# Products with values issued for four exponent steps at a time, in a fused attention and feed-forward layer

## What is computed

```python
qkv = x @ Wqkv + bqkv                      # 16 query heads of 16, 4 key/value heads of 16
scores = einsum('bqhd,bkhd->bhqk', q, k) / HD
prob = softmax(scores)
out = einsum('bhqk,bkhd->bqhd', prob, v).reshape(b, s, D)
x = layernorm(x + out @ Wout + bout)
gate, up = split(x @ ternary(w_gate_up).T) # 1024 hidden features
h = rms_norm(silu(gate) * up)
x = layernorm(x + h @ ternary(w_proj).T)
```

## Time and profile before

| | us |
|---|---|
| median of 3 runs | 574.95 (574.88 to 575.57) |
| the profiled execution's own time | 574.5 |
| its span, first to last instruction | 571.8 |
| PE busy in it | 528.4 (92%) |
| DVE busy | 455.4 (80%) |
| ACT busy | 374.2 (65%) |
| POOL busy | 319.5 (56%) |

### The profile page before, as it was taken

One profiled execution on the slowest core, in us unless ns is written; L12 is line 12 of the kernel. 1 busy time (PEld: TensorE's weight loads), 2 busy tenths in 40 slices (PEclk: granted clock), 3 DMA queues, 4 the chain that ended last, 5 costly groups with the idle time before them and its releaser, 6 DMA issues.

```text
span 571.8 us, 13792 instructions
## 1 busy us (share of the span) xinstructions
PE 528.4 (92%) x4176; PEld 444.7 (78%) x4176; DVE 455.4 (80%) x1025; ACT 374.2 (65%) x754; POOL 319.5 (56%) x478
## 2 busy tenths in 40 slices
PE   6497999999999999999999999999999999999883
PEld 5386778778888787878888888878887877787772
DVE  6878877788888888888888887888898888885764
ACT  5456755666767767676776776776767676667663
POOL 5577671255645555555646564556555565466764
PEclk9899999999999999999999999999999999999998
DMA  7865444343333426062534444261606253010001
GB/s 229 144 142 95 86 95 104 74 91 88 84 95 93 105 68 128 19 160 26 128 69 102 93 94 100 79 116 56 134 6 166 29 125 71 12 44 6 19 20 37
DMA packets 53931, 49.05 MB, mean 86 GB/s; under 512 B 6144, under 2 KB 53888, under 8 KB 53888
## 3 DMA queue, kind: packets, MB, share of 16 engines
q1 hardware_dynamic: 53200, 48.13, 38.2%
q10 hardware_dynamic: 688, 0.39, 0.2%
HBM read 33.29 MB, written 14.68 MB: 84 GB/s over the span
## 4 chain that ended last, share of the span: by engine, by line
PE 63%; DVE 20%; issue 7%; POOL 4%; ACT 2%; DMA 2%; SPq 0%; DVEq 0%; ACTq 0%; POOLq 0%
PE ffn_ps L551 19%; PE short_ps L477 10%; PE pv_ps L579 8%; PE short_ps L523 8%; PE down_ps L564 7%; PE exp_ps L532 6%; DVE row_max L800 5%; DVE gated L863 3%; DVE h_f L870 3%; PE short_ps L587 2%; DVE attB L902 2%; DVE pvT L896 1%; DVE w_hat L833 1%; POOL sq_sum L966 1%; DVE w_sum L821 1%
## 5 line engine op out<-in xcount | busy, mean ns | idle before, releaser
L800 DVE TENSOR_REDUCE row_max<-short_ps 128x2 f32<-128x512 f32 x256 | 173.4, 681 | 67.2 <-PE short_ps L523 66.8
L961 POOL TENSOR_TENSOR h_lo<-h_f,h_hi 128x256 fp32r<-128x256 f32 x128 | 94.8, 740 | 206.9 <-ACT h_hi L698 206.8
L722 ACT ACTIVATE probs<-exp_ps 128x1024 f32<-128x1024 f32 x128 | 130.7, 1021 | 34.1 <-PE exp_ps L532 33.2
L523 PE MATMUL short_ps<-k_st,q_st 65*128 65x256 f32 x512 | 108.2, 294 | 9.3 <-DVE v_ones L919 6.2
L523 PEld LDWEIGHTS short_ps<-k_st,q_st 65*128 65x128 f32 x512 | 87.9, 192 | 20.7 <-issue 7.8
L707 ACT ACTIVATE tanh<-ffn_ps 128x256 f32<-128x256 f32 x120 | 45.5, 380 | 85.2 <-PE ffn_ps L551 85.2
L551 PE MATMUL ffn_ps<-x1T_hi,wguT 128*128 128x256 f32 x480 | 82.0, 293 | 10.3 <-DVE h_f L870 8.9
L564 PE MATMUL down_ps<-wpT,h_hi 128*128 128x256 f32 x256 | 78.7, 330 | 3.8 <-POOL h_lo L961 3.8
L532 PE MATMUL exp_ps<-q_st,k_st 67*128 67x512 f32 x256 | 80.7, 397 | 0.8 <-DMA q_st<-shift_lo 0.6
L551 PEld LDWEIGHTS ffn_ps<-x1T_hi,wguT 128*128 128x128 f32 x480 | 64.8, 189 | 19.3 <-issue 9.7
L966 POOL TENSOR_TENSOR sq_sum<-sq_sum,h_sq 128x256 f32<-128x256 f32 x105 | 79.5, 758 | 0.0
(11 more groups left out here) (102 smaller groups left out, 830.7 us busy)
## 6 DMA issues: line engine op xcount, KB each, us to landing
q_st<-q_dram SPq DMA_DIRECT2D x128, 128.0 KB, 4.1
q_dram<-q_p SPq DMA_DIRECT2D x16, 512.0 KB, 3.0
xn<-in_L_attn_x_dram SPq DMA_DIRECT2D x16, 256.0 KB, 3.4
k_st<-k_dram SPq DMA_DIRECT2D x64, 64.0 KB, 2.8
res<-in_L_attn_x_dram SPq DMA_DIRECT2D x16, 256.0 KB, 2.9
out_dram<-y_out SPq DMA_DIRECT2D x16, 256.0 KB, 2.9
wgu_raw<-in_L_ffn_w_gate_up_dram SPq DMA_DIRECT2D x8, 256.0 KB, 6.6
k_dram<-k_p SPq DMA_DIRECT2D x16, 128.0 KB, 2.4
```

The source lines that it names most:

```text
L523: last = pe.matmul(bank[:, t * S:(t + 1) * S], q_st[0:PAD, st.par, head, t * P:(t + 1) * P], k_st[0:PAD, st.par, st.s % 4, :], start=True, ...
L722: act.activation(probs[:, st.s % 4], exp_ps[:], ACT.Exp).then_inc(exp_done, 1)
L800: dve.tensor_reduce(row_max[:, st.par, head * TT:(head + 1) * TT], short(n, f"max{i}")[:].rearrange("p (t k) -> p t k", t=TT), AX.X, ALU.m ...
L961: pool.tensor_tensor(h_p[1][:, st.s % 4, :], h_f[:, st.s % 2, :], h_p[0][:, st.s % 4, :].bitcast(F32), ALU.subtract).then_inc(h_lo, 1)
```

## The change

`probs` gets eight buffers, one for each step of a sequence. `times_v` is called at s = 3 and s = 7 only and does the work of four steps in one go: first steps s-3 and s-2, then s-1 and s, each as before. The products of steps 0 and 1 move from position 1 to position 3, those of steps 4 and 5 from position 5 to position 7. The semaphore `pv_done` counts two calls for each sequence in place of four, and the waits on it are rewritten for that. To make room on chip, eight buffers of the feed-forward and output stages (`tanh`, `gated`, `h_f`, `h_sq`, `y_sb`, `r2` and the two of `y_out`) are laid into `wgu_raw`, which held the weights as they were read.

```diff
-        probs = sb("probs", [P, 4, TT, 2, S])
+        probs = sb("probs", [P, SLOTS, TT, 2, S])
-        tanh = sb("tanh", [P, 2, S])
-        gated = sb("gated", [P, 2, S])
-        h_f = sb("h_f", [P, 2, S])
+
+        tanh, gated, h_f, h_sq, y_sb, r2, y_even, y_odd = (wgu_raw[:, 2 * i:2 * i + 2, :] for i in range(8))
+        y_out = (y_even, y_odd)
@@ times_v
-                if st.s % 4 == 1:
-                    wait(pe, pv_turned, st.count(2, st.s // 4))
-                for t in range(TT):
-                    for s in (st.s - 1, st.s):
-                        for i in range(2):
-                            r = 32 * quadrant(s % 4, i)
-                            last = pe.matmul(pv_ps[r:r + 32, s % 4 // 2, :], v_ones[:, st.par, t, s % 4, :],
-                                             probs[:, s % 4, t, i, :], start=(t == 0), stop=(t == TT - 1),
-                                             tile_position=(0, r))
+                wait(pe, pv_turned, st.count(2, st.s // 4))
+                for first in (st.s - 3, st.s - 1):
+                    for t in range(TT):
+                        for s in (first, first + 1):
+                            for i in range(2):
+                                r = 32 * quadrant(s % 4, i)
+                                last = pe.matmul(pv_ps[r:r + 32, s % 4 // 2, :], v_ones[:, st.par, t, s % 4, :],
+                                                 probs[:, s, t, i, :], start=(t == 0), stop=(t == TT - 1),
+                                                 tile_position=(0, r))
                 last.then_inc(pv_done, 1)
@@ PE's slot
-                if (st := n.chunk(PV0)) and st.s % 2:
+                if (st := n.chunk(PV0)) and st.s % 4 == 3:
                     times_v(st)
@@ ACT's slot
-                    wait(act, pv_done, st.count(4, st.s // 2 - 1))
-                    act.activation(probs[:, st.s % 4], exp_ps[:], ACT.Exp).then_inc(exp_done, 1)
+                    wait(act, pv_done, st.count(2, st.s // 4 - 1))
+                    act.activation(probs[:, st.s], exp_ps[:], ACT.Exp).then_inc(exp_done, 1)
@@ DVE's slot
-                        wait(dve, pv_done, st.count(4, 2 * half + 2))
+                        wait(dve, pv_done, st.count(2, half + 1))
-                    wait(dve, pv_done, st.count(4, -4))
+                    wait(dve, pv_done, st.count(2, -2))
```

More of the change, by code:

```diff
@@ L274, in postln_layer @@
         x1T = [sb(f"x1T_{n}", [P, 2, DT, S], F32R) for n in ("hi", "lo")]
-        tanh = sb("tanh", [P, 2, S])
-        gated = sb("gated", [P, 2, S])
-        h_f = sb("h_f", [P, 2, S])
+        tanh, gated, h_f, h_sq, y_sb, r2, y_even, y_odd = (wgu_raw[:, 2 * i:2 * i + 2, :] for i in range(8))
+        y_out = (y_even, y_odd)
         h_p = [sb(f"h_{n}", [P, 4, S], F32R) for n in ("hi", "lo")]
-        h_sq = sb("h_sq", [P, 2, S])
         sq_sum = sb("sq_sum", [P, 2, S])
-        y_sb = sb("y_sb", [P, TT, D])
         ms = sb("ms", [P, TT])
         inv = sb("inv", [P, TT])
-        r2 = sb("r2", [P, TT, D])
         st2 = sb("st2", [P, TT, 6])
@@ L290, in postln_layer @@
         mean2 = sb("mean2", [P, TT])
-        y_out = sb("y_out", [P, 2, TT, D])
         exp_ps = ps("exp_ps", [P, TT, 2 * S])
@@ L450, in slot @@
                     sp_wait(y_done, st.count(TT, TT))
-                    sp.dma_start(out[st.seq()].rearrange("(t p) d -> p t d", p=P), y_out[:, st.par]
+                    sp.dma_start(out[st.seq()].rearrange("(t p) d -> p t d", p=P), y_out[st.par]
                                  ).then_inc(stored[st.par], 16)
@@ L712, in slot @@
                     for t in range(TT):
-                        act.activation(y_out[:, st.par, t, :], r2[:, t, :], ACT.Identity, bias=shift2[:, t:t + 1],
+                        act.activation(y_out[st.par][:, t, :], r2[:, t, :], ACT.Identity, bias=shift2[:, t:t + 1],
                                        scale=rstd2[:, t:t + 1]).then_inc(y_done, 1)
```

## The result

The changed kernel takes 602.4 us (599.57 to 602.7, 4 runs) where the kernel before takes 574.91 in the same rounds: slower by 4.6%, ratio 1.046, 95% interval 1.0434 to 1.0485. The forecast was 598.4 with a range from 588 to 603. The profiled execution took 602.7, its span is 600.0, so 28.2 more than the span before.

The account below looks back on a forecast made before the run. PE bounds most of the cycle, DVE two stretches per sequence (from max0 at positions 4 and 0). 20.7 - 1.2 + 2.9 + 1.0 = 23.4 on the profiled 574.5 gives 597.9; with 0.45 for the median, 598.4, range 588 to 603.

Parts of the forecast that it names:

- The steady state: Twelve sequences, 100 to 475 us: 24 additions of 0.86 at positions 3 and 7, +20.7; 1.2 back at position 1.
- What PE itself saves: Per pair of calls merged, PE needs 2.06 us in place of 2.40, so 0.34 less for each of 32 pairs.
- rival A: PE's saving shows because DVE's stretches are not the bound: 10.9 us less, 564.1; chance 5%.
- The last sequences: Slots 128 on: four additions, 3.4 us, less 0.5 back at one gate; sum 2.9, bounds 1.5 and 3.4.
- The first 97 us: Four pairs before the steady state: 1.0 us more, the middle between -1.4 and 3.4.
- no DMA moves: Under edits counted at nothing: later calls are covered by DVE's idle time, none needed from ACT or SP, DMAs unmoved.
- the forecast's own range: 594 to 602 us, from errors in the prologue, last sequences and steady state, before opening it to rivals.
- rival C: The ends of merged calls don't merge: each addition costs 1.00, 3.9 us more, 602.3; chance 10%.
- D: Longer PE waits at positions 5 and 1 each bring a gate step at half the clock: 28 us more, 626; chance 2%.
- 1.2 us less of DVE: Loss DVE would need in each of its two stretches for PE's saving to show; 1.2 us or more.
- The drain at a change of the array's mode: Skill's rule: tiling mode changes drain the engine; half go away, 11 us faster if PE's time alone counted; sum made without it.
- The signs named beforehand: Profile after: calls 1.86 us, cycle about 32.5, PE's h_f waits some 30, DVE idle about 2.1 at positions 4 and 0.

Follow-up runs that it names:

- half0_only: Changed kernel, but only each sequence's first half is done in one call (position 3); the second keeps calls at positions 5 and 7: 587.75 us, ratio 1.023.
- half1_only: Changed kernel, but only each sequence's second half is done in one call (position 7); the first keeps calls at positions 1 and 3: 587.48 us, ratio 1.0209.
- light_act_after: Changed kernel without nearly all of PV_NORM, and ACT's writing of x1 and output cut to 16 of 256 columns: 569.52 us; kernel before, cut likewise, 569.34.
- busy31: Changed kernel with seven more products in slot 31, where PE waits for the shift rows; their result is overwritten: 600.49 us, ratio 1.0439.
- light_norm_after: Changed kernel with nearly all of PV_NORM's work left out: 580.45 us, ratio 1.0083 to the kernel before with the same cut.
- pairs_first2: Changed kernel, but the first two sequences keep their four calls each: 597.54 us, ratio 1.0396.
- max_later_6: Kernel before, with DVE at position 6 writing gated and h_f first and taking the maximum of max0 after them: 578.02 us, ratio 1.0035.

## Why the prediction was right, and where it was wrong

*The steady state.* From the gate of slot 32 to that of slot 128, the kernel after takes 392.81 us and the one before 372.99: 19.8 more. The forecast had 20.7 - 1.2 = 19.5. The length of the call (1.86), the additions at positions 3 and 7 (0.87 for 0.86), what came back at position 1 (0.16 for 0.15) and nothing at position 5 all came as worked out. Confirmed by half0_only and half1_only, each on its own. What PE itself saves was mis-sized: 1.20 is the price of a call at position 3, and at positions 5 and 1 the calls gave back 1.04 and 1.10 (light_act_after). The forecast didn't need this number, only rival A did.

*The last sequences.* 3.0 more from slot 128 to the end, against 2.9: +0.86 to 0.88 at the four calls, and 0.54 back at one slot, where I had 0.5.

*The first 97 us, with slot 31.* Forecast 1.0, bounds -1.4 and 3.4; measured 5.35 up to the gate of slot 32 (106.59 against 101.24). This is the step that failed: 4.35 of the 4.8 us between the profiled execution and the forecast for it (602.7 and 597.9). Its bounds were made from PE's work alone. Of the 5.35, 1.36 had come by slot 31, and 0.8 of these is missing in busy31, the same program up to there, whose stretch at 1.2 GHz near 46 us is shorter; so that part is more likely the clock's than the change's. In slot 31 itself are 3.98: 0.87 for the call, about 1.4 from the clock during it, and 1.6 more of waiting for the shift rows than before. DVE wrote those rows 1.75 later than before, behind the late max0 of slot 28, and their transfer took 3.82 us from issue to landing. In the kernel before, by the list of DMA issues in the same stretch, it was 2.6:

```profile
q_st<-shift_lo SPq DMA_DIRECT2D x1, 8.0 KB, 2.6
```

Since slot 31 itself started 1.36 later, the late issue makes only 0.4 of the 1.6; the other 1.2 is the longer transfer. It took 3.2 to 3.8 in the changed kernels (half1_only, busy31, light_norm_after and light_act_after too) and 1.9 to 3.0 in those that keep the first sequences' calls at position 5 (also half0_only, pairs_first2, max_later_6); why is not shown. The text had said that no DMA moves. None is moved in the program, but one is issued by what DVE does behind a moved call, and it ended on the path.

*The margin.* 602.4 lies outside the forecast's own range of 594 to 602 and inside the given one only because that was opened up to rival C, whose mechanism didn't occur. That the time is inside is in part luck.

*The rivals.* C (the ends don't merge, 602.3) has nearly the measured time and is still wrong: the calls are 1.86. D (the clock) may be right that a longer wait can bring the lower level, and is wrong on place and size: not at positions 5 and 1 of each cycle, where the clock stays at 1.00, but once, for some 1.4 us. A (PE's saving shows) was refuted, and more thoroughly than I had argued: even with PV_NORM's work cut, light_norm_after is slower than its base, since at position 5 ACT's queue comes next, and with ACT lightened too, PE has little to gain, 0.2 a pair. I had named 1.2 us less of DVE as the point from which A decides; PV_NORM is 1.44 shorter in light_norm_after at position 4 (0.78 from its first step to the one behind it, against 2.22), so that point was wrong. The drain at a change of the array's mode, of which the Trainium skill's page TensorEngine Tiling (Array Packing) speaks in its section Tiling Modes, is less with half of the changes gone, by 0.34 for a pair by the rows of position 3 and by some 0.2 as measured; it was worth nothing here because PE waited in those places anyway.

*The signs named beforehand.* The cycle grew to 32.53 (32.5), DVE's idle time at position 4 to 2.17 (2.1), the stretch stayed at 6.1. At position 0 the idle time ahead of max0 grew to 1.32 only, the rest being ahead of the copy of v. PE's waits for DVE grew to 23.3, where I had said some 30 for `h_f`, and 14.8 of them stand at the transposes ahead of the gate. A stretch below 1.00, a sign of D, did come, in slot 31.

## What to carry to other kernels

Before work is merged into one group, ask for each piece which stretch it leaves and which it enters: a piece that leaves a stretch where its engine waits anyway gives nothing back, and the whole of it is paid where it arrives. Where engines hand work round in each step, read the length of each step and what its shortest version is; an engine's total over two steps hides that each has a least length of its own, and removing the first bound shows the second (here DVE, then at one position ACT's queue, then PE itself to within 0.1 us). Look for the wait that remains in every version, and for what stands ahead of the releasing instruction in its engine's queue: moving one maximum behind the two steps that release PE made the kernel 0.5% faster.

## What the runs showed of the hardware

A call of 16 records in four column strips takes 1.00 us and one of 32 takes 1.86, so a batch of four costs 0.215 and the rest is paid once for each call, beside 0.10 on each side at position 3. What a call costs depends on its neighbours: taken out from between scores and the turned maxima, it gave back 1.04 and 1.10 and not 1.20.

After a wait of PE of 0.90 and of 1.56 us ahead of the long call, the granted clock was at 1.2 GHz for most of the call, which then took 3.55 and 3.27. After waits of 0.62 and 0.65 it stayed at 2.4 GHz, and neither the steady state's waits of 0.84 before the transposes nor one of 0.95 ahead of a gate (at 104.33, kernel before) brought the lower level. What tells them apart is open.
